# A rotary step on ten features instead of 128: the shuffle-and-rotate chains of q and k replaced by products and one multiplication

## The reference

```
ct_q  = x @ w_down_q.T + b_down_q            # 192 wide
ct_kv = x @ w_down_kv.T + b_down_kv          # 64 wide
q = (ct_q  @ w_up_q.T + b_up_q) + rope(ct_q  @ wq_r.T + bq_r)
k = (ct_kv @ w_up_k.T + b_up_k) + rope(ct_kv @ wk_r.T + bk_r)
v = ct_kv @ w_up_v.T + b_up_v
rope(y)[2i]   = y[2i]*cos_i - y[2i+1]*sin_i
rope(y)[2i+1] = y[2i]*sin_i + y[2i+1]*cos_i
tn_i = 1 / (10000 ** (2i) / 256);  angle = position * tn_i
```

## Time and profile before

| | us |
|---|---|
| median of 3 runs | 498.13 (497.07 to 499.1) |
| span of the profiled execution, first to last instruction | 497.5 |
| PE busy in it | 441.3 (89%) |
| DVE busy | 265.3 (53%) |
| ACT busy | 187.8 (38%) |
| POOL busy | 164.6 (33%) |

### The profile page before, as it was taken

One profiled execution on the slowest core, in us unless ns is written; L12 is line 12 of the kernel. 1 busy time (PEld: TensorE's weight loads), 2 busy tenths in 40 slices (PEclk: granted clock), 3 DMA queues, 4 the chain that ended last, 5 costly groups with the idle time before them and its releaser, 6 DMA issues.

```text
span 497.5 us, 7909 instructions
## 1 busy us (share of the span) xinstructions
PE 441.3 (89%) x2503; PEld 287.1 (58%) x2504; DVE 265.3 (53%) x638; ACT 187.8 (38%) x383; POOL 164.6 (33%) x237
## 2 busy tenths in 40 slices
PE   3657789999999998979899999999999999998791
PEld 2445556676766664646467565666666666665461
DVE  4555657878787867673866621222222222235665
ACT  1425466666666665545522222222222222211110
POOL 1325445555555545122220011111112110038533
PEclk9977899999999998888999999999999999999996
DMA  8542236363636363601275500111111111124311
GB/s 259 140 68 70 76 78 189 78 198 81 193 80 193 86 192 92 193 3 44 75 229 194 159 21 27 48 55 42 42 42 42 45 47 55 42 75 116 106 42 63
DMA packets 53718, 48.27 MB, mean 97 GB/s; under 512 B 5846, under 2 KB 49366, under 8 KB 53686
## 3 DMA queue, kind: packets, MB, share of 16 engines
q1 hardware_dynamic: 47152, 39.17, 27.1%
q0 software_dynamic: 1872, 5.11, 3.8%
q10 hardware_dynamic: 4662, 3.59, 2.5%
HBM read 25.72 MB, written 9.31 MB: 70 GB/s over the span
## 4 chain that ended last, share of the span: by engine, by line
PE 64%; DVE 14%; POOL 8%; issue 6%; DMA 3%; ACT 2%; SPq 2%; POOLq 0%; DVEq 0%; ACTq 0%
PE bank L1248 45%; PE bank L1252 7%; PE bank L1366 4%; PE bank L1382 4%; PE bank L1330 3%; DVE nmax L987 3%; POOL pv L642 2%; SPq L427 2%; DMA stacks<-parts_q 2%; DVE wall L1017 1%; DVE stats_at L896 1%; POOL x_sb L591 1%; POOL rstd_at L528 1%; DVE wall L1007 1%; POOL stacks L674 1%
## 5 line engine op out<-in xcount | busy, mean ns | idle before, releaser
L1248 PE MATMUL bank<-wall,stacks 128*128 (+2 forms) x616 | 211.4, 486 | 6.3 <-DVE stacks L1181 4.4
L1248 PEld LDWEIGHTS bank<-wall,stacks 128*128 128x128 f32 x616 | 111.1, 190 | 69.0 <-issue 59.3
L987 DVE TENSOR_REDUCE nmax<-bank 128x2 f32<-128x512 f32 x128 | 85.2, 686 | 41.1 <-PE bank L1330 40.9
L1177 DVE TENSOR_TENSOR stacks<-stacks,bank 128x512 f32<-128x512 f32 x39 | 26.7, 686 | 84.0 <-PE bank L1248 84.0
L1330 PE MATMUL bank<-stacks 96*128 96x256 bf16 x256 | 50.3, 285 | 15.4 <-DVE nmax L987 8.0
L626 POOL DMA_INDIRECT stacks<-x_sc,row_i x23 | 22.0, 955 | 124.3 <-PE bank L1252 124.3
L837 ACT ACTIVATE stacks<-bank 128x512 f32<-128x512 f32 x39 | 23.3, 597 | 81.8 <-PE bank L1248 78.3
L1382 PE MATMUL bank<-stacks 99*128 99x256 bf16 x256 | 50.9, 282 | 1.2 <-ACT wall L799 1.0
L1181 DVE COPY stacks<-bank 128x512 f32<-128x512 f32 x39 | 26.9, 691 | 46.5 <-PE bank L1252 46.1
L799 ACT ACTIVATE pv<-bank 128x512 f32<-128x512 f32 x64 | 37.9, 595 | 36.3 <-PE bank L1382 35.8
L799 ACT ACTIVATE wall<-bank 128x512 f32<-128x512 f32 x64 | 37.8, 599 | 28.7 <-PE bank L1382 26.8
(11 more groups left out here) (168 smaller groups left out, 529.1 us busy)
## 6 DMA issues: line engine op xcount, KB each, us to landing
wall<-gate_up SPq DMA_DIRECT2D x8, 1024.0 KB, 5.8
stacks<-parts_k SPq DMA_DIRECT2D x96, 64.0 KB, 2.6
stacks<-parts_q SPq DMA_DIRECT2D x91, 64.0 KB, 2.6
wall<-down SPq DMA_DIRECT2D x8, 512.0 KB, 7.2
y_exp<-stacks ACTq DMA_DIRECT2D x23, 128.0 KB, 1.7
x_tok<-wall SPq DMA_DIRECT2D x8, 256.0 KB, 2.7
stacks<-x_tok SPq DMA_DIRECT2D x16, 128.0 KB
out<-stacks SPq DMA_DIRECT2D x8, 256.0 KB
```

The source lines that it names most:

```text
L987: dve.tensor_reduce(nmax[:, half, qt, 2 * pair:2 * pair + 2], two(sm_bank[u % 2]), AX.X, ALU.max, negate=True).then_inc(sm["sm_max"], 1)
L1177: dve.tensor_tensor(hid, sg, fu[:, :], ALU.mult).then_inc(sm["h_sb"], 1)
L1248: last = pe.matmul(out_ap, lhsT, rhs, start=(n == 0), stop=(n == len(pairs) - 1))
```

## The change

Instead of turning all 128 features of m = 0, the changed kernel turns the ten that have an angle. In the setup the ten columns are taken out of the turning weights and biases ("unturned"), so that the rest can be added to the plain weights, for both m. The ten columns, and the same ten with neighbours swapped, form a new weight of 128 columns (20 for q, 20 for k, the others zero): `w_rope`. Per batch:

- A_R (PE, slot 0): two products with `w_rope` into w0. It has 128 rows and columns although 40 of the columns carry something.
- A_T (DVE, slot 1): one instruction adds the bias and multiplies by a table that holds cos in some rows and signed sin in others.
- A_Q (PE, slot 1): the first of the two products of q for both m, into w1.
- A_QK (PE, slot 3): the second for both m, k's two, and two products with a matrix of zeros and ones that put the turned rows on their features, added in PSUM.
- A_ev0, A_ev1 (ACT, slots 5 and 6): four copies of q and k with their biases.

That is ten products. The shuffles, POOL's rotations and DVE's two additions are no longer there. M1 goes from slot 1 to slot 2 on PE and ACT. The load of `w_rope` is one more transfer ahead of w_q's. Prologue and row 0 are written anew to match.

```diff
-        NLOAD = 2
+        NLOAD = 3
-        MOVED = {"A_k0": 2, "A_kswap": 2, "A_q0": 2, "A_q0r": 3, "A_qswap": 4, "M1": 4, "A_krot": 4, "A_qrot": 5, "A_kadd": 6,
-                 "A_qk1": 8, "A_khigh": 8, "A_qhigh": 8, "A_qadd": 8, "N_v": 9,
+        MOVED = {"A_R": 2, "A_T": 2, "A_Q": 3, "A_QK": 4, "M1": 4, "A_ev0": 6, "A_ev1": 6,
+                 "A_khigh": 8, "A_qhigh": 8, "N_v": 9,
...
-                    (0, "B_ct A_ones A_k0 A_kswap A_krot A_q0 A_q0r A_qswap F_qrot"),
+                    (0, "B_ct A_ones A_R A_T A_Q A_QK"),
...
-                    (1, "A_q0r A_qswap"),
+                    (1, "A_QK"),
                     (2, "B_xnT"),
                     (0, "S4 S5 S6 S7 M0"),
-                    (1, "F_qrot A_kadd A_qadd F0_khigh F0_qhigh F0_kres F0_qres F0_kmid F0_qmid F0_klow F0_qlow"),
-                    (1, "A_stack A_qk1 F1_khigh F1_qhigh F1_kres F1_qres"))
+                    (1, "A_ev0 F0_khigh F0_qhigh F0_kres F0_qres A_ev1 F0_kmid F0_qmid F0_klow F0_qlow"),
+                    (1, "A_stack F1_khigh F1_qhigh F1_kres F1_qres"))
...
+            sp.dma_start(wrp_sb[:, :, :], w_rope.rearrange("(k p) n -> p k n", p=P)).then_inc(sm["attn_w"], 16)
...
-            order = {0: ("M1",), 2: ("A_krot",), 3: ("A_qrot",), 6: ("B_power",), 8: ("A_kres", "M0",),
+            order = {0: ("M1",), 6: ("B_power",), 8: ("A_kres", "M0",),
...
+            def qk_copy(m):
+                def f(b, par):
+                    if m == 0:
+                        if b == 0:
+                            act.wait_ge(sm["bias_sum"], 1)
+                        act.wait_ge(sm["qk_ps"], b + 1)
+                        if counted(b):
+                            act.wait_ge(sm["kl"], split_of(b - 1))
+                            act.wait_ge(sm["ql"], split_of(b - 1))
+                    act.activation(kf[:, m, :], two(w0)[:, m, :], ACT.Identity, bias=bcol[:, 4 + m:5 + m]
+                                   ).then_inc(sm["k_sb"], 1)
+                    act.activation(qf[:, m, :], two(w1)[:, m, :], ACT.Identity, bias=bcol[:, 2 + m:3 + m]
+                                   ).then_inc(sm["q_sb"], 1)
...
+            def rope(b, par):
+                dve.wait_ge(sm["r_ps"], b + 1)
+                if counted(b):
+                    dve.wait_ge(sm["qk_ps"], b)
+                dve.scalar_tensor_tensor(rope_t[:, :], w0[:, 0:S], bcol[:, 10:11], cst[:, C_ROPE:C_ROPE + S],
+                                         ALU.add, ALU.mult).then_inc(sm["rope_sb"], 1)
...
-            order = {0: ("E_xn2",), 1: ("A_kswap",), 2: ("A_kadd",), 3: ("A_qswap",), 5: ("E_router", "B_stats",),
-                     6: ("D_div0", "A_qadd",), 8: ("D_div1", "B_norm",), 9: ("N_v",), 11: ("D_y",),
+            order = {0: ("E_xn2",), 1: ("A_T",), 5: ("E_router", "B_stats",),
+                     6: ("D_div0",), 8: ("D_div1", "B_norm",), 9: ("N_v",), 11: ("D_y",),
...
+            def a_qk(b, par):
+                pe.wait_ge(sm["rope_sb"], b + 1)
+                for m in range(2):
+                    pe.matmul(two(w1)[:, m, :], wq_sb[:, 1, P * m:P * m + P], ctT[par][:, 1, :],
+                              start=False, stop=(m == 1), skip_group_check=True)
+                    pe.matmul(two(w0)[:, m, :], wkv_sb[:, P * m:P * m + P], ctT[par][:, 1, :],
+                              start=(m == 0), stop=(m == 1), skip_group_check=True)
+                pe.matmul(two(w1)[:, 0, :], cst[:, C_SEL:C_SEL + P], rope_t[:, :],
+                          start=False, stop=True, skip_group_check=True)
+                pe.matmul(two(w0)[:, 0, :], cst[:, C_SEL + P:C_SEL + 2 * P], rope_t[:, :],
+                          start=False, stop=True, skip_group_check=True).then_inc(sm["qk_ps"], 1)
...
-            order = {0: ("A_k0",), 1: ("M1", "A_q0",), 2: ("E_xn2T", "A_q0r",), 4: ("E_router",), 5: ("A_qk1",),
+            order = {0: ("A_R",), 1: ("A_Q",), 2: ("M1", "E_xn2T",), 3: ("A_QK",), 4: ("E_router",),
```

More of the change, by code:

```diff
@@ L76, in constants @@
     tn[inside] = np.float32(1.0) / (np.float32(10000.0) ** exps[inside] / np.float32(D))
-    assert not tn[P // 2:].any()
+    assert not tn[ROT // 2:].any()
     ang = np.outer(np.arange(S, dtype=np.float32), tn).astype(np.float32)
     cos, sin = np.cos(ang), np.sin(ang)
-    for row, f in enumerate(head_minor(np.arange(P))):
-        t[row, C_COS:C_COS + S] = cos[:, f // 2]
-        t[row, C_SIN:C_SIN + S] = sin[:, f // 2] * (1 if f % 2 else -1)
+    for n, top in enumerate(SIDE.values()):
+        for f in range(ROT):
+            t[top + f, C_ROPE:C_ROPE + S] = cos[:, f // 2]
+            t[top + ROT + f, C_ROPE:C_ROPE + S] = sin[:, f // 2] * (1 if f % 2 else -1)
+            for r in (f, ROT + f):
+                t[top + r, C_SEL + P * n + HT * f] = 1.0
     t[:, C_DESC:C_DESC + E] = E - np.arange(E)
@@ L757, in f @@
                 def f(b, par):
[L758 to L761 removed]
+                    act.wait_ge(sm[f"{k}_sb"], 2 * b + m + 1)
                     if b == 1:
@@ L1285, in a_k0, with a_q @@
                 if b == 1 or b == 2:
-                    pe.wait_ge(sm["qk1_sb"], 2 * b)
+                    pe.wait_ge(sm["k_sb"], 2 * b)
                 pe.wait_ge(sm["ct_sb"], 2 * b + 2)
-                for r in range(2):
-                    last = products(two(w0)[:, r, :], [(wkv_sb[:, D * r:D * r + P], ctT[par][:, 1, :])])
-                last.then_inc(sm["k0_ps"], 1)
-            def q0_half(b, par, r):
-                last = products(two(w1)[:, r, :], [(wq_sb[:, k, D * r:D * r + P], ctT[par][:, k, :])
-                                                   for k in range(KT)])
-                if r == 1:
-                    last.then_inc(sm["q0_ps"], 1)
-            def a_q0(b, par):
+                products(w0[:, 0:S], [(wrp_sb[:, k, :], ctT[par][:, k, :]) for k in range(KT)]
+                         ).then_inc(sm["r_ps"], 1)
+            def a_q(b, par):
+                if b == 0:
+                    pe.wait_ge(sm["bias_sum"], 1)
                 if b == 1:
@@ L1449, in d_router @@
                 last.then_inc(sm["rt_ps"], 1)
-            steps = {"B_xnT": a_xnT, "B_ct": a_ct, "B_ct1": lambda b, par: ct_half(b, 1), "A_k0": a_k0, "A_q0": a_q0,
-                     "A_q0r": lambda b, par: q0_half(b, par, 1), "A_qk1": a_qk1, "N_v": a_v,
+            steps = {"B_xnT": a_xnT, "B_ct": a_ct, "B_ct1": lambda b, par: ct_half(b, 1), "A_R": a_rope, "A_Q": a_q,
+                     "A_QK": a_qk, "N_v": a_v,
                      "SM": sm_scores, "M0": lambda b, par: m_turn(b, par, 0),
```

158 lines of the change are left out of this document (53 added, 105 removed).

## The result

Slower. The changed kernel's median is 507.46 us (505.86 to 510.85, 4 runs) beside 498.62 for the kernel before (4 runs): a ratio of 1.0194, with a 95% interval from 1.0148 to 1.024. Two later measurements of the same two kernels gave less: 505.54 beside 499.21, 1.0112 [1.003, 1.0194] (4 and 13 runs), and 504.32 beside 499.42, 1.0101 [1.0066, 1.0135] (12 and 17 runs). The forecast of 502.3 had the sign right and the size too small: 507.46 lies above its range of 497.5 to 506.0, the two later medians lie inside it.

What follows compares the result with a forecast made beforehand. PE was taken to set the attention's pace, DVE next. Row 1 0.8, rows 2 to 4 3 x 0.80, row 5 0.58, row 6 0.4, start 0: +4.2 us, 502.3 for the median, range 497.5 to 506.0.

Steps and rivals of the forecast that it cites:

- Steady rows: Rows 2 to 4 of the attention: slot 10 starts at 16.83 instead of 16.03, +0.80 us for each row.
- M1's wait: PE in a steady row: the 1.09 us wait for POOL's split goes as M1 moves to slot 2.
- this point decides, since DVE's unbroken stretch starts there: Slot 5's score product for DVE, 1.20 us later, sets when DVE's unbroken work up to slot 10 begins.
- Row 5 and row 1: Row 5, without B_norm, is bound by PE: +0.58 us; row 1: +0.8, bounded by 0.4 and 1.3.
- Row 6: M1 stands next to E_xn2T here too: ACT's 0.37 us copy and its signal cost +0.4 us.
- the start and row 0: Program start and first row: row 0 can give back later transfers; taken as 0, bounded by -1.3 and +1.8 us.
- the wait at 74.05: PE's wait for batch 2's DMA, said with batch 2's split at 61.84 to end row 0.
- M0, put 1.1 later: Start: M0's transpose comes up to 1.73 us later behind batch 1's six products; 1.1 taken.
- Batch 1's first transfer by SP, put 1.8 behind: Start: batch 1's copies follow M0's DMA on ACT, so its DMAs, 41.72 before, start about 1.8 us later.
- The load of the new weights: Setup: 128 KB load and longer weight additions, put at nothing, bounded by 0 and 0.7 us.
- The clock as a rival: Rows with two new waits could bring half-clock stretches: one row 505.5 us, four rows 515; chance 0.06.
- The rule of the shared port: DVE stands still while GpSimd holds the SBUF ports: some 0.5 us a row saved, total 500.7; not followed.

Runs made afterwards that it cites:

- e1: Changed kernel with DVE's statistics for batch r+3 (B_stats) in slot 3 instead of slot 5: 505.86 us, 1.0147 of the kernel before.
- e5: Changed kernel, statistics in slot 3, logits in slot 4, M1 in slot 1, A_ev0 ahead of batch 1's copy in the start: 498.64 us, 0.9987 of before.
- f3: e5 (its four moves) plus idle products on PE in the start, 10 behind v, 3 and 6 later: 494.48 us, 0.9909 of the kernel before.
- f1: Kernel before plus idle products, read by nobody, where PE waits in the start: 496.95 us, 0.9937 of the kernel before.
- f2: Changed kernel with the idle products of f1 and 6 more behind M0: 501.09 us, 1.0031 of the kernel before.

## Where the forecast held and where it failed

*Steady rows: right in size, half right in cause.* M1's wait went, E_xn2T waits 0.60 (0.67 forecast), avT0 0.52 (0.52), DVE idles 3.45 and then works without a break; rows 2 to 4 cost +0.90 each (+0.80). But "this point decides, since DVE's unbroken stretch starts there" is half the truth: e1 took some 1.2 us out of that stretch (138.94 to 140.18 above) and the row gave back 0.17. PE's chain (a product more, two waits) is as long as DVE's, and only e5, which shortens both, brings the row back.

*Row 5 and row 1:* +0.7 (+0.58) and +0.5 (+0.8). *Row 6:* -0.7 for +0.4. Row 6 also has stretches at half clock whose length differs from execution to execution: 6.9 us in the first profile of before, over half of it in the earlier trace rows, about 2 in the changed kernel's, of which the first begins in row 5:

```profile
204.40:207.80 3.40, 3.40 (x24) 1.44 (x25) 2.26 (x8) 0.47 (x1) 1.79 (x5) 0.50 0.43 108
```

Where both kernels have 1.8 to 2.1 us of it in row 6, the row takes 22.55 and 22.58 before and 22.52, 22.43 and 22.30 after. The wait behind M1 that was priced is there (0.55, where the second profile of before waits 0.23 for DVE), but a later wait for DVE's reduce is shorter by as much (0.83 for 1.21), so the row pays nothing for it.

*The step that failed is the one on the start and row 0: "I take 0, bounded by -1.3" below and by +1.8 above.* The first pair has +4.2 to row 1's start (77.41 less 73.20), the four profiles +2.9. Two things in it were wrong.

First, row 0 does not give the delay back. The third profile of before and f3 run the whole of row 0 at full clock:

```profile
45.13:73.65 28.52, 22.98 (x175) 15.15 (x175) 19.14 (x38) 18.41 (x40) 15.25 (x27) 1.00 0.34 85
```

```profile
40.37:70.45 30.08, 23.75 (x177) 15.61 (x177) 18.27 (x33) 18.16 (x40) 11.94 (x22) 1.00 0.33 85
```

That is 1.56 more, and with the 0.36 of f1 and f2 some 1.9 at row 1's start: an estimate, since f3 has the four moves as well, and it is the upper bound and not the 0 that was chosen. (f1 and f2 alone give 1.3, with the lower clock in f1's row 0.) Row 0 waits for batch 1's transfers in both kernels, 1.39 us in that profile of before and 2.32 in f3. And the wait at 74.05 that was to end row 0 lies behind row 1's first product (73.20); in the changed kernel it is gone.

Second, the clock. What is left, 1.0 of the 2.9 and 2.3 of the 4.2, goes with it. The prediction wrote "more if the slow clock of that stretch lasts" and priced nothing: in the changed kernel PE's work of batch 1 (32.07 to 36.3) runs at 0.50 of the clock, behind the wait of 7.35 us for the first transfers; in f2, where products fill that wait, it keeps 1.00. That stretch lasts 10.2 us in three profiles of the changed kernel, and 6.8 in its other one and in all four of before. So M0, put 1.1 later, comes 4.4 later in the first pair (39.58 and 43.94; the pace of the first products is part of it) and 0.35 later in f1 and f2 (38.08 and 38.43). Batch 1's first transfer by SP, put 1.8 behind before's 41.72, comes 5.1 behind it, and 1.1 behind it in f1 and f2 (40.12 and 41.22):

```profile
46.82 1.19 SPq L434 DMA_DIRECT2D stacks<-parts_k  x2
```

The load of the new weights, put at nothing, cost nothing that shows: at the fast pace the first products of q and k start at 13.19 before and at 13.01 after.

*The clock as a rival* was looked for in rows 1 to 4, where it kept 1.00, and given 0.06. It fell elsewhere: in the start, and behind row 7, where seven of the eight profiles have it late in the program and the first of before happened not to (3.2 of the 9.4 us). The sum was made on that one execution, the shortest span of four. How often an execution of either kernel has which pace in its first products stays open: four profiles of each show both.

The Trainium skill (TensorE: Matmul & The Clock Gate, "Part 1: The HAM clock gate") says that how many products run slow at a kernel's beginning changes from run to run of the same kernel, and puts the loss below 1% of a span. This case agrees: 0.92 and 0.47 us a product in two executions of the changed kernel, and a start of row 0 between 45.07 and 47.15, 2.1 of some 504 us.

The rule of the shared port that the prediction weighed was tried there on the wrong instruction: it is about DVE instructions with two inputs in SBUF, and the reduce of the earlier trace rows, 0.69 in both kernels, reads PSUM. DVE's norms are of that kind. Before, B_norm's run beside POOL's work and take 0.48 each (137.06); D_yn's, of the same form, have POOL idle beside them and take 0.48 each (144.8): the trace does not show the rule there either.

## What to carry to other kernels

Where two engines take turns through a row, taking work from one or moving one wait shows its worth only if the other chain gets shorter too: look for the second-longest chain before pricing a move, and test moves together as well as singly. Profile the unchanged kernel more than once before making a sum on it: differences of 2 to 3 us in the start and the tail belonged to the execution, while the rows between came again within 0.01 us. Where the matrix engine waits ahead of work that others wait for, products that nobody reads can shorten the program: by some 2 to 3 us on the kernel before (f1) and some 4 on the changed one (f2, and f3 against e5), beside some 6 for the better order of e5.

## What the runs showed of the hardware

- The granted clock's column is 1.00 for the first 25 us in all eight profiles of the two unchanged kernels, though the products there take 0.92 us in some executions and 0.43 to 0.47 in others: the trace has no record of the clock ahead of 11.5 to 17.8 us, so there the column is no measurement, and the distance between products is what to read. In this window of the changed kernel's second profile two products of A_R and two of A_Q took 3.5 us:

```profile
13.47:17.00 3.53, 3.51 (x9) 2.85 (x10) 0.48 (x1) 0.00 (x0) 0.00 (x0) 1.00 0.79 279
```

- A wait of 2.06 us near the end was followed by eight products in 1.99 us, at full pace; waits of 3.3 to 3.8 us in the same place, in seven profiles, by eight products in 2.84 to 3.78, all or in part at 0.50 of the clock: such a wait cost more than its length.
- Taking 4.1 us of work a row from POOL left DVE's reduce at 0.69 us and ACT's exponential at 0.60.
